# Moving ScalarE's gather copies behind weight splits, an early turn of the last pass, and two closing strips

## What is computed

```python
# mixture 1: E, K, F = 8, 2, 1536, and a shared expert
comb = zeros(T, E).at[arange(T), top_idx].add(top_s)         # two experts per token
for wg, wu, wd, c in (Wg, Wu, Wd, comb.T):
    acc = acc + c[:, None] * (silu(x @ wg.T) * (x @ wu.T) @ wd.T)
out = acc + silu(x @ sg.T) * (x @ su.T) @ sd.T
# mixture 3: E, K, H = 8, 2, 3072, no shared expert
h = silu(x @ Wg[e].T) * (x @ Wu[e].T)
out = out + h @ Wd[e].T * w_e[:, None]
```

## Time and profile before

| | |
|---|---|
| median of 3 runs | 1276.29 us (1274.68 to 1277.39) |
| the profiled execution | 1276.04 us |
| its span, first to last instruction | 1274.3 us |
| PE, DVE, ACT busy | 90%, 39%, 30% of the span |
| mean granted clock of TensorE | 0.964 of full speed |
| chain that ended last | PE 54%, DMA 31%, DVE 9%, ACT 3% |
| mixture 1, by the trace | about 280 to 595 us |
| mixture 3, by the trace | about 717 to 1271 us |

### The profile page before, as it was taken

One profiled execution on the slowest core, in us unless ns is written; L12 is line 12 of the kernel. 1 busy time (PEld: TensorE's weight loads), 2 busy tenths in 40 slices (PEclk: granted clock), 3 DMA queues, 4 the chain that ended last, 5 costly groups with the idle time before them and its releaser, 6 DMA issues.

```text
span 1274.3 us, 15593 instructions
## 1 busy us (share of the span) xinstructions
PE 1142.1 (90%) x6431; PEld 694.6 (55%) x6431; DVE 497.3 (39%) x805; ACT 384.6 (30%) x442; POOL 22.0 (2%) x47
## 2 busy tenths in 40 slices
PE   5999999888899999978899789989899898989887
PEld 4677686666755455534755645445445445544533
DVE  7977542446743333202522442233123123412310
ACT  4866312233733232100212152223123123312310
POOL 2000000000000000000000000000000000000000
PEclk9999999999899999999999879989899998989899
DMA  9988646736789999999510199999999999999996
GB/s 374 424 340 342 262 165 245 319 149 268 277 363 426 425 425 425 424 426 425 231 33 25 72 429 424 425 424 426 424 425 426 426 425 425 425 426 425 426 425 258
DMA packets 43301, 443.77 MB, mean 348 GB/s; under 512 B 4848, under 2 KB 5008, under 8 KB 8672
## 3 DMA queue, kind: packets, MB, share of 16 engines
q1 hardware_dynamic: 40320, 427.05, 80.5%
q0 software_dynamic: 2912, 15.74, 3.2%
HBM read 442.38 MB, written 0.39 MB: 347 GB/s over the span
## 4 chain that ended last, share of the span: by engine, by line
PE 54%; DMA 31%; DVE 9%; ACT 3%; issue 2%; SPq 0%; POOL 0%; DVEq 0%; ACTq 0%
DMA ring<-in_weights 20%; DMA scratch<-in_weights 11%; PE PJ L1661 10%; PE AC L1687 6%; PE TP L1708 5%; PE AC L1480 4%; PE PJ L1648 3%; PE PJ L1650 3%; PE PJ L1649 3%; PE AC L1492 3%; PE PJ L1396 2%; DVE ring_lo L1141 2%; PE MS L1373 2%; PE PJ L1453 1%; PE TP L1614 1%
## 5 line engine op out<-in xcount | busy, mean ns | idle before, releaser
L1661 PE MATMUL PJ<-ring,picked 128*32 128x512 f32 (+1 forms) x888 | 188.7, 596 | 9.4 <-DMA ring<-in_weights 6.0
L1661 PE MATMUL PJ<-scratch,picked 128*64 128x512 f32 (+1 forms) x480 | 106.9, 594 | 5.4 <-DMA scratch<-in_weights 5.3
L1141 DVE TENSOR_TENSOR ring_lo<-ring,w_lo_u 128x1536 fp32r<-128x1536 f32 x36 | 62.2, 1755 | 113.3 <-ACT w_lo_u L756 113.2
L1661 PEld LDWEIGHTS PJ<-ring,picked 128*32 128x32 f32 (+1 forms) x888 | 55.6, 122 | 90.3 <-issue 89.8
L1123 DVE SCALAR_TENSOR_TENSOR act<-low,CB,PJ 128x512 f32<-128x512 f32 x48 | 35.7, 744 | 173.9 <-PE PJ L1650 93.9
L1661 PE MATMUL PJ<-extra,picked 128*64 128x512 f32 (+1 forms) x360 | 87.1, 599 | 3.8 <-DMA extra<-in_weights 2.9
L1141 DVE TENSOR_TENSOR ring_lo<-ring,w_hi_u 128x1536 fp32r<-128x1536 f32 x34 | 58.6, 1754 | 81.3 <-ACT w_hi_u L756 81.2
L739 ACT ACTIVATE low<-PJ 128x512 f32<-128x512 f32 x48 | 28.3, 591 | 202.1 <-PE PJ L1661 152.7
L1708 PE MATMUL TP<-ring,extra 128*64 128x512 f32 (+3 forms) x528 | 85.8, 487 | 2.8 <-DMA scratch<-in_weights 1.4
L756 ACT ACTIVATE w_hi_u<-ring 128x1536 fp32r<-128x1536 f32 x34 | 49.1, 1481 | 118.0 <-DMA ring<-in_weights 106.9
L1708 PE MATMUL TP<-scratch,extra 128*64 128x512 f32 (+2 forms) x496 | 80.5, 488 | 2.9 <-issue 2.9
(11 more groups left out here) (375 smaller groups left out, 1875.3 us busy)
## 6 DMA issues: line engine op xcount, KB each, us to landing
ring<-in_weights SPq DMA_DIRECT2D x156, 1536.0 KB, 29.0
scratch<-in_weights SPq DMA_DIRECT2D x79, 1536.0 KB, 32.1
extra<-in_weights SPq DMA_DIRECT2D x34, 1536.0 KB, 33.6
extra<-in_attn POOLq DMA_DIRECT2D x12, 768.0 KB, 9.3
extra<-in_attn POOLq DMA_DIRECT2D x6, 512.0 KB, 8.7
extra<-in_weights SPq DMA_DIRECT2D x8, 384.0 KB, 24.9
scratch<-in_ffn_vectors POOLq DMA_DIRECT2D x1, 2688.5 KB, 12.1
extra<-in_x SPq DMA_DIRECT2D x1, 384.0 KB, 3.0
```

The source lines that it names most:

```text
L1141: v.tensor_tensor(slab_lo(n)[:, half * HALF:(half + 1) * HALF], half_slab(n, half), hi_half(n, half).bitcast(F32), ALU.subtract).then_inc( ...
L1661: ins = mm(dst[c], x[:, t, c], slab_at(LOAD[q, kind, side])[:, t * SEG:(t + 1) * SEG], start=(t == 0), stop=(t == KT - 1))
```

## The change

1. In mixture 1, ACT's copy `gather(0)` moves from ahead of the splits of pass 1's g and u slabs to behind them, and `gather(2)` moves in the same way behind the splits of pass 2's. `gather(1)` stays.
2. `count_chosen` is called before the third column tile of g0 instead of the fifth.
3. Ten warming matmuls (`keep_warm(10, ...)`, 128x128, result not used) follow the router product in both mixtures.
4. The hidden rows of pass 47 get a tile of their own (`low[1]`, by the new function `hT_of`) and are turned before d46.
5. The last two slabs are loaded in two strips of 1536 columns each instead of four of 768; PE waits before the first and the third quarter.

```diff
+        def hT_of(q):
+
+            if q == LAST_PASS[3]:
+                return low[1]
+            return hT if PASSES[q][0] == "pair" else hTh
...
-                for t in range(4):
+                for t in range(2):
                     for n, index in closing:
-                        part = slice(t * D, (t + 1) * D)
+                        part = slice(t * HALF, (t + 1) * HALF)
...
-                    A(hT if PASSES[q][0] == "pair" else hTh, TP[:, 0:SEG], ACT.Copy).then_inc(S("hT_ready"), 1)
+                    A(hT_of(q), TP[:, 0:SEG], ACT.Copy).then_inc(S("hT_ready"), 1)
...
                     silu_of(q)
-                    if l == 1 and q == 0:
-                        gather(0)
                     if q > m["first"]:
                         hidden_turned(q - 1)
                     if l == 1 and q == 1:
                         gather(1)
-                        gather(2)
                     if l == 1 and q == 2:
                         shares_turned()
                     whole_hi(q + 1, "g")
                     whole_hi(q + 1, "u")
+                    if l == 1 and q == 0:
+                        gather(0)
+                    if l == 1 and q == 1:
+                        gather(2)
...
                 ins.then_inc(S("router_product"), 1)
+                keep_warm(10, PJ[:, 0:P])
...
-                            if between and t == 4:
+                            if between and t == 2:
                                 between()
...
-                        if q == LAST_PASS[3]:
-                            pe.wait_ge(S(f"closing_landed_{t}"), 32)
+                        if q == LAST_PASS[3] and t % 2 == 0:
+                            pe.wait_ge(S(f"closing_landed_{t // 2}"), 32)
...
-                                ins = mm(Y[c, a:b], hT[:, t * P:(t + 1) * P][:, c],
+                                ins = mm(Y[c, a:b], hT_of(q)[:, t * P:(t + 1) * P][:, c],
...
+                    if l == 3 and q == end:
+                        turn_hidden(end)
                     if q > first:
                         down(q - 1)
...
-                turn_hidden(end)
+                if l == 1:
+                    turn_hidden(end)
```

## The result

The changed kernel takes 1264.01 us (median of 4 runs, 1263.08 to 1264.71) beside 1275.49 us for the kernel before (4 runs, 1273.95 to 1277.39): 11.5 us less, a ratio of 0.9909 with a 95% interval of 0.9892 to 0.9926. The forecast was 1265.2 us. In a later series beside other kernels it took 1263.24 us (5 runs, 1263.03 to 1264.91). The profiled execution took 1263.08 us, its span is 1261.3 us.

What follows compares the result with a forecast made beforehand. Bound: mixtures' gapless 425 GB/s weight streams, mixture 1's started by the end of d2. 1274.3 - 9.8 (7.1 + 2.7, mixture 1) - 1.3 (end) = 1263.2 us span, 1265.2 us measured; range 1262.0 to 1270.0 us.

Steps and rivals of the forecast that it cites:

- What bounds the kernel: Mixtures 1 and 3: gapless 425 GB/s weight stream; PE's end of d2 sets mixture 1's start, each microsecond earlier arrives whole.
- Parts 1 and 2: Mixture 1 up to g1: DVE's waits of 1.05 us (count) and 1.89 us (ACT's split) go, g1 starts 2.94 us earlier.
- The warming matmuls: Behind both router products: ten take 1.3 us at full clock and cost nothing; at half clock mixture 3 loses up to 0.9 us.
- Part 3: Mixture 1, g1 to g2: with g1 kept at 5.8 us, g2 starts at 317.1 instead of 324.20 us, 7.1 us earlier.
- the term that I had left open, g1's clock: g1's 18 matmuls: 4.2 us at full clock, 7.7 at half, 5.8 taken; bounds 1.6 us better, 1.9 us worse.
- the favourable bound: g1 in mixture 1 at full clock, 4.2 us instead of 5.8: 1.6 us better, 11.4 us up to d2.
- Part 3's other condition: Ahead of g2 in mixture 1: its second half is ready at 314.8 us, with 2.3 us to spare.
- Part 4: g2 in mixture 1: with no gap ahead it runs at full clock, 4.17 instead of 6.84 us, 2.67 us more.
- Part 6: Kernel's end: turn and copy hidden, d47 follows d46 at 1262.10 instead of 1263.38 us; 1.28 us, bounds 0.6 and 1.3.
- The strips' wait: At d47: second strip has 0.5 us left; landing up to 1.2 us later would cost 0.7 us of the gain.
- the row at 399 GB/s: Stretch where 384 KB strips move, 399 against 425 GB/s: longer strips could gain at most 0.5 us for 3.1 MB.

Runs made afterwards that it cites:

- both delays: Changed kernel plus 90 warming matmuls in mixture 1, in one kernel ahead of d2 (1283.8 us), in another ahead of d10 (1267.02 us).
- the late turn: Changed kernel with the last pass's hidden rows turned behind d46 again, own tile and two strips kept: 1265.14 us (one run).

## Why the prediction was right

**What bounds the kernel** held: 20.1 us at the end of d2 are 19.8 us at the end, and 20 us ahead of d10 are 3, where I had put work inside the stream at nothing.

**Parts 1 and 2** were forecast as g1 2.94 us earlier; it was 3.01 us. The gap left ahead of g1, 2.37 us, was forecast as 2.3. But 1.05 us of it hang on the execution that the rows were read from. I read the wait of 1.05 us as the place of the count. It needs the half clock of g0 as well: with the count in its old place and g0 at full clock the wait is 0.19 us, and with ACT's order alone it is none; with the count early it is none at half clock either. So the earlier count is a guard for executions in which g0 runs at half clock, and worth next to nothing in the others.

**The warming matmuls** were mis-sized. I took 1.3 us for ten, from a row of eight records; these are twenty records and 2.5 us (2.26 us up to the start of g0). They fill the wait of 1.58 us for the low part and run over it by 0.6 us. In mixture 1 this is hidden, as I had it. In mixture 3 the counting products start 3.68 us behind the router product instead of 3.21. My range held 0.9 us for that. It cost nothing: the counting products end at 710.9 us, and DVE, which takes the count, is busy with the low part of the tokens until 711.06 us. SP's first load comes 7.57 us behind the router product in both kernels.

**Part 3** forecast g2 7.1 us earlier with g1's clock as before, and it was 8.99. The difference is the term that I had left open, g1's clock: g1 took 4.23 us, the favourable bound, and not 5.8. Keeping the 5.8 us of before was a choice and not a forecast of the clock; that the favourable bound came is luck, since two other kernels with the same gap had g1 at 5.8 us. Part 3's other condition, that the second half of g2 is ready in time, held: g2 has no gap.

**Part 4**, the clock in g2, gave 2.59 us; forecast 2.67. So the sum up to d2 was 11.58 us against 9.8 in the forecast and 11.4 at its upper bound. The 1.6 us are g1's clock and the rest is small.

**Part 6** forecast 1.28 us, and the turn gave 1.47. I had let d47 start when d46's busy time of 5.38 us is over; the records of consecutive matmuls overlap (0.39 us each, 0.23 us apart in g1), and the distance of the starts is 5.18 us. The strips' wait, which I had as a bound of 0.7 us, didn't come: the second strip landed 0.4 us before its use, close to the 0.5 us that I had worked out, and the longer strips changed nothing. But I read the row at 399 GB/s wrongly. It is the beginning of a fall that goes on until the stream ends, and its 94% say little of how fast strips of 384 KB move: from 1254 to 1264 us the kernel before has 298 GB/s and a DMA share of 0.75, about as much as the changed kernel in its last 10 us with strips of 768 KB. The share is the mean over the 16 engines and falls with the rate, from which I take that some engines are done while others still move data; no view here lists them one by one. That the length doesn't matter is shown by the pair with four and with two strips, and not by that row. The changed kernel's 336 GB/s above are the same fall.

**The size.** The profiled spans differ by 13.0 us, the medians by 11.5, and the forecast was 11.1. So the forecast lies nearer to the median than to the profile on which its sum was made, and a part of that closeness is luck: on the pair of profiles the sum is 1.9 us short, most of it g1's clock. The profiled execution of the changed kernel is the fastest of its four, and the median of the kernel before fell from 1276.29 to 1275.49 us with its fourth run. The nine times of the changed kernel lie in two groups, 1263.03 to 1263.37 us and 1264.67 to 1264.91 us, with nothing between. The distance, 1.3 to 1.9 us, fits g1 partly at half clock (1.5 to 1.6 us), as two kernels with the same gap had it. That would explain it, but only two executions of the changed kernel were traced, both of the first group and with g1 at full clock. This stays open.

## What to carry to other kernels

A stage that is bound by a stream of fixed length, as mixture 1 is here, has one instant that counts most, the one at which the stream can run for good; look for the last long wait of the loading queue, ask what its releaser waited for, and expect little from savings behind it (here 20 us of delay there cost 3). In an in-order queue, a small copy that waits for a late producer costs what stands behind it: here two copies of 0.8 us held up 10 us. Before an edit is credited with a wait that it removes, compare a second execution: a wait of a microsecond may be there only at one level of the clock.

## What the runs showed of the hardware

- The same gap leads to different clocks. Behind 2.33 to 2.37 us without a matmul, g1 ran at 2.4 GHz in six profiles (both of the changed kernel, ACT's order alone, both delays, the late turn) and partly at 1.2 GHz in two (the count in its old place and four strips, 5.8 us instead of 4.2). Behind 1.58 us, g0 was at full clock with ACT's order alone and partly at half in the kernel before and without the warming. Behind 4.2 us, the clock was down each time: in g1 and g2 of both kernels that have such gaps. Half clock in a part of a slab cost 1.5 to 1.6 us behind the short gap and 1.5 to 2.6 us behind the long one.
- An fp32 matmul of 128x128 is two records and takes 0.225 to 0.23 us (90 in 20.3 us, and ten in 2.26 us up to the next start).
- Behind a full queue the length of the closing strips decides nothing: four of 768 KB (the changed kernel), issued from 1216.5 to 1218.1 us, landed 28.8 to 34.6 us later, eight of 384 KB (four strips again), issued from 1219.6 to 1237.8 us, 16.6 to 29.4 us later, and PE waited for none.
- A stream doesn't end at its full rate. In steps of 2 us from 1244 us the changed kernel's runs at 421, 344, 243 and 156 GB/s, with DMA shares of 1.02, 0.83, 0.58 and 0.39; over the last 10 us it is 307 GB/s with strips of 768 KB and 299 with strips of 384 KB.
